# The high and low parts of one portion's first layer, made by GpSimd

## The reference

```
a = x_t @ Wx + b + h @ Wh;   i, f, o = sigmoid(...), g = tanh(...)
c = f * c + i * g;   h = o * tanh(c)              # 64 steps, one after another
z = relu(s0 * [h, -h] @ sign(k0)) * 2             # 512 -> 1024
z = relu(s1 * z @ sign(k1)) * 2                   # 1024 -> 1024
out = x + s2 * z @ sign(k2)                       # 1024 -> 256
```

## Time and profile before

| | |
|---|---|
| runs | 275.78 median, 275.46 to 276.33 |
| the profiled execution: span | 274.2 us; its records give no time beside the span |
| mean granted TensorE clock | 1.000 |
| TensorE matmul busy | 268.8 us, 98% |
| VectorE busy | 219.3 us, 80% |
| ScalarE busy | 174.3 us, 64% |
| GpSimd busy | 40.7 us, 15%, 62 instructions |

### The profile page before, as it was taken

The page is one execution under the profiler, slowest core; times in us unless marked ns, Lnnn a source line. Parts: engine busy times, 40 slices in busy tenths (PEclk is TensorE's granted clock), DMA queues, the critical chain, the costliest instruction groups (busy, mean ns, idle before and its releaser), DMA issues.

```text
span 274.2 us, 8895 instructions
## 1 busy us (share of the span) xinstructions
PE 268.8 (98%) x3568; PEld 219.2 (80%) x3568; DVE 219.3 (80%) x777; ACT 174.3 (64%) x522; POOL 40.7 (15%) x62
## 2 busy tenths in 40 slices
PE   8999999999999999999999999999999999999995
PEld 5887888788999998999988999998777677655663
DVE  3878888888888888888887888886888787998355
ACT  4798787878566666556756565667677667733320
POOL 0010000022111124211311101000200004703030
PEclk9999999999999999999999999999999999999999
DMA  7980000000000001000010001000100000100003
GB/s 199 337 352 1 4 2 0 2 4 2 2 2 1 4 2 41 2 2 5 5 39 0 4 2 41 2 2 5 41 0 2 2 4 0 41 0 0 2 0 115
DMA packets 5432, 8.72 MB, mean 32 GB/s; under 512 B 656, under 2 KB 3472, under 8 KB 5264
## 3 DMA queue, kind: packets, MB, share of 16 engines
q1 hardware_dynamic: 5104, 7.64, 8.2%
q10 hardware_dynamic: 288, 0.52, 0.6%
HBM read 6.07 MB, written 2.10 MB: 30 GB/s over the span
## 4 chain that ended last, share of the span: by engine, by line
PE 85%; DVE 7%; ACT 5%; DMA 1%; issue 1%; ACTq 0%
PE WK L533 27%; PE WK L516 14%; PE G L495 10%; PE WK L551 9%; PE G L486 9%; PE ACC L565 6%; PE G L551 4%; PE WK L582 2%; ACT tT L790 2%; DVE aT L1009 2%; PE ACC L582 1%; DMA x<-in_x 1%; PE G L516 1%; DVE xw L848 1%; ACT xw L688 1%; PE ACC L516 1%
## 5 line engine op out<-in xcount | busy, mean ns | idle before, releaser
L533 PE MATMUL WK<-h,k 128*128 128x256 f16 (+1 forms) x856 | 107.7, 276 | 0.0
L533 PEld LDWEIGHTS WK<-h,k 128*128 128x128 fp8e5 x856 | 80.8, 98 | 10.8
L790 ACT ACTIVATE tT<-aT 128x128 f32<-128x128 f32 x126 | 38.9, 310 | 46.8 <-DVE aT L1009 45.1
L1009 DVE TENSOR_REDUCE aT<-G 128x128 f32<-128x256 f32 x128 | 48.1, 417 | 5.7 <-PE G L495 4.2
L677 ACT ACTIVATE G<-xw 128x256 f32<-128x256 f32 x126 | 46.7, 370 | 0.0
L516 PE MATMUL WK<-xs,wxs 128*128 128x512 f32 x168 | 42.5, 400 | 0.0
L486 PEld LDWEIGHTS G<-h,w 128*128 128x128 f16 x1008 | 32.0, 96 | 10.7 <-DVE h L1026 9.6
L495 PE MATMUL G<-h,w 128*128 128x64 f16 x1008 | 39.5, 192 | 0.0
L486 PE MATMUL G<-h,w 128*128 128x32 f16 x1008 | 35.3, 177 | 1.2 <-DVE h L1026 0.9
L516 PEld LDWEIGHTS WK<-xs,wxs 128*128 128x128 f32 x168 | 30.4, 188 | 5.9
L495 PEld LDWEIGHTS G<-h,w 128*128 128x128 f16 x1008 | 33.2, 97 | 0.0
(11 more groups left out here) (116 smaller groups left out, 281.0 us busy)
## 6 DMA issues: line engine op xcount, KB each, us to landing
x<-in_x SPq DMA_DIRECT2D x3, 512.0 KB, 8.5
out_y<-x SPq DMA_DIRECT2D x10, 128.0 KB, 1.8
xw<-in_wh SPq DMA_DIRECT2D x4, 256.0 KB, 5.2
k<-in_k SPq DMA_DIRECT2D x1, 1024.0 KB, 10.4
out_y<-x SPq DMA_DIRECT2D x4, 192.0 KB, 1.9
x<-in_x ACTq DMA_DIRECT2D x2, 256.0 KB, 3.7
xw<-in_wx SPq DMA_DIRECT2D x4, 128.0 KB, 4.1
xw<-in_wx SPq DMA_DIRECT2D x2, 256.0 KB, 5.4
```

The lines of the kernel that those rows point to most:

```text
L533: ins = eng.matmul(layer_src(tile), w, rhs, start=a == 0, stop=last)
L790: eng.activation(tT[:, B * j0:B * j1], aT[:, j0:j1].rearrange("p j b -> p (j b)"), ACT.Tanh, scale=half_gain0 if t == 0 else half_gain).th ...
L1009: eng.tensor_reduce(aT[:, j0:j1], G[g][:, 0:256].rearrange("p (j h b) -> p j b h", h=2, b=B), op=ALU.add, axis=AX.X).then_inc(added[g])
```

## The change

For the eight first-layer tiles of portion 5, ScalarE reads the bank once, for r1 in f32, and nothing else reads it. GpSimd makes from r1 the high part (a copy to f16) and then the low part (r1 less the high part). TensorE's products p1 and p2 wait for the new semaphore r1_lo, and the next owner of a bank waits for r1_made. In the planner such a tile counts as emptied when it is finished, its pair stands in GpSimd's list one step later, and p1 and p2 are ready from the step after that. In GpSimd's list of step 53 the pairs of tiles 0 and 1 stand behind the two y additions. The pair waits for r1 alone, not for a point of the recurrence.

```
-            inputs = (0, N1, a // 2) in emptied
+            inputs = (0, N1, a // 2) in paired
-            inputs = (0, N1, 4 + a // 2) in emptied and ("p1", tile[1]) in emptied
+            inputs = (0, N1, 4 + a // 2) in paired and ("p1", tile[1]) in emptied
...
+        paired.update(pool[t])
         for tile, at in finished:
-            if tile[0] in ("x", "p1", "y"):
+            if tile[0] in ("x", "p1", "y") or tile[:2] == (0, N1):
                 emptied.add(tile)
-            if tile[0] == "y":
+            if tile[0] == "y" or tile[:2] == (0, N1):
                 pool[t + 1].append(tile)
...
-                    e.wait_ge(lo_made[0], 8 * N1 + 4 * (q - 1) + k + 1)
+                    e.wait_ge(r1_lo, 4 * (q - 1) + k + 1)
...
+                elif old[0] == 0 and old[1] == N1:
+                    e.wait_ge(r1_made, old[2] + 1)
...
                     eng.activation(r1[:, m], layer_src(tile), ACT.Relu).then_inc(r1_made)
+                    return
...
+            def r1_pair(m):
+
+                eng.wait_ge(r1_made, m + 1)
+                eng.tensor_copy(b1[:, m, 0], r1[:, m]).then_inc(r1_hi)
+                eng.wait_ge(r1_hi, m + 1)
+                eng.tensor_tensor(b1[:, m, 1], r1[:, m], b1[:, m, 0], ALU.subtract).then_inc(r1_lo)
+
             for t in range(T):
                 if 0 <= t - MIX_STEP < MIXES:
                     mix_part(t - MIX_STEP)
-                for _, c, mo in pool_plan[t]:
-                    eng.wait_ge(hl_made, t + 1)
-                    y_add(c, mo)
+                for kind, c, m in pool_plan[t]:
+                    if kind == "y":
+                        eng.wait_ge(hl_made, t + 1)
+                        y_add(c, m)
+                    else:
+                        r1_pair(m)
```

More of the change, by code:

```diff
@@ L151, in make_plan @@
     emptied = {("x", 0, j) for j in range(NJ)}
-    todo = []
+    todo, paired = [], set()
     ahead = 0.0
@@ L387, in lstm_ffn @@
         acc_mm, y_out, y_made = ([sem(f"{n}{mo}") for mo in range(2)] for n in ("acc_mm", "y_out", "y_made"))
-        mixed, r1_made, p1_made, n2_mm, r12_made, hi22, lo22 = (
-            sem(n) for n in ("mixed", "r1_made", "p1_made", "n2_mm", "r12_made", "hi22", "lo22"))
+        mixed, r1_made, r1_hi, r1_lo, p1_made, n2_mm, r12_made, hi22, lo22 = (
+            sem(n) for n in ("mixed", "r1_made", "r1_hi", "r1_lo", "p1_made", "n2_mm", "r12_made", "hi22", "lo22"))
         prod_mm = {q: sem(f"prod_mm{q}") for q in range(1, 8)}
```

## The result

The changed kernel has a median of 278.0 us (277.32 to 278.15, four runs) beside 275.7 for the kernel before on the same chip: a ratio of 1.007, 95% interval 1.0054 to 1.0086. It is 0.7% slower. 276.3 was forecast for the likeliest case, with 274.2 to 277.7 as the range; the ratio puts the time at the range's upper end, the bare median 0.3 above it.

The account below looks back on a forecast made before the run. TensorE bounds the kernel, with 2.2 us of waits for the recurrence in steps 53 to 60. Gains of 2.25 less GpSimd's hold-ups in steps 54 and 59 gave 28.1 against 27.6, +0.5: 276.3 us, range 274.2 to 277.7.

Parts of the forecast that it names:

- the case with the largest chance of its own: The main forecast for the whole kernel: a small loss, 276.3 us, own range 275.5 to 277.0, chance 0.50.
- slow cast: Steps 56 to 58: with GpSimd's cast at 0.59 us, L1018 comes 0.1 late, at most +0.3 over the steps.
- The gain: Steps 53 to 60: work taken from VectorE and ScalarE saves 2.25 us if GpSimd's work were free.
- A pair's length: GpSimd's cast (0.48), wait on its own semaphore (0.06) and subtraction (0.92) cost 1.46 us, at most 1.6.
- One pair in a step hidden: Steps 56 to 58, pairs 3 to 5: L1015 is blocked for 0.3 us, but L1018 waits for its tanh anyway.
- Step 54: GpSimd's queued pairs hold up VectorE's recurrence instructions in turn: effective length 5.1 us, +1.84 over 3.26.
- rival (A): Step 54: all six recurrence instructions lose to GpSimd's six; 6.0 us, kernel 277.5 with the +0.3; chance 0.28.
- Step 59: Pairs 6 and 7 ready together; the second holds L1018 and L1020: 4.1 us, +0.9 over 3.20, bounds 3.8 and 4.15.
- (B): Casts don't hold VectorE up, subtractions do; step 54 at 3.7, step 59 at 3.55, kernel 274.3; chance 0.12.
- (C): GpSimd's pairs cost the recurrence nothing in any step: -2.25 us, kernel 273.5; chance 0.10.
- The place at 14.22: Trace of before: L843 takes 1.07 us against 0.68 beside GpSimd casts, read as casts holding VectorE up.

Follow-up runs that it names:

- e1: The changed kernel with GpSimd's eight pairs left out, so p1 and p2 multiply zeros: 273.68 us, ratio 0.9925 to the kernel before.
- e6: The changed kernel with pairs 0 to 6 one per step, none in step 54, tile 7's parts made as in the kernel before: 273.87 us, ratio 0.9914.
- e9: The changed kernel with two one-column memsets between each pair's cast and subtraction: 275.49 us, ratio 0.9986 to the kernel before, on another chip.
- e8: The changed kernel with 15 matmuls of zeros in TensorE's two waits of step 55: 276.95 us, ratio 1.0032 to the kernel before.
- e5: The kernel before, nothing taken away, with GpSimd's eight pairs added into a spare tile nobody reads: 279.91 us, ratio 1.0142.
- e7: The changed kernel as it is, measured a second time: 277.40 us, ratio 1.0052 to the kernel before.
- e2: The changed kernel with each GpSimd pair replaced by three memsets that read nothing: 273.82 us, ratio 0.9928 to the kernel before.

## Why the prediction came out as it did

The forecast was a small loss, hardly to be told from none (+0.5 us); the measured loss is three to four times that (0.5 and 0.7% of 276). The mechanism was right, and the order of chances too (slower 0.42, the largest); the size was not, and the case with the largest chance of its own (0.50, 275.5 to 277.0) isn't the one that came. The top of its range isn't added up: 5.1, 4.15 and the 0.3 of a slow cast give 276.6.

- The gain, -2.25: e1 has 25.39 for the 25.4 forecast, and -2.2 us in its median. TensorE's order was unchanged, as followed in the prediction: `make_plan` of both kernels gives the same list for TensorE in every step, and both traces have 3,568 matmuls.
- A pair's length, 1.46: the cast took 0.50 (0.48 assumed), the subtraction 0.91, from 193.55 to 195.04 in all 1.49. The next pair's cast begins 0.05 ahead of that end.
- One pair in a step hidden: right. Pairs 4 and 5 lie in steps 57 and 58, which take no more than TensorE's need, and L1019 loses at most 0.1. Pair 3 fell into the long step 55 here; e6 has it in a step of its own, at no cost.
- Step 54, the term that failed in size. The prediction wrote 5.1 and named 6.0 for the case in which L1026 loses too; I had it and the subtraction within 0.05 us and gave rival (A) 0.28. Measured is rival (A) in every one of its six turns: 191.82 to 198.06, less the 0.41 at which the second half belongs, 5.83. e9 shows how near such a race is: 0.08 us of delay turned that of L1024. The rows of before could have settled it: a held-up VectorE instruction ends about 0.08 behind GpSimd's and the next starts 0.03 later, 0.11 in all, while GpSimd's wait on its own semaphore was put at 0.06 and took 0.08. I had these figures and still let VectorE win the one race that mattered.
- Step 59: 4.1 forecast, 3.90 measured. L1024 takes 0.96, as forecast, but ends at 3.30 of the step in place of 3.49: the two pairs came 0.2 earlier, the first cast at 0.29 for 0.45, the second at 1.73 for 1.93.
- Not in the sum, nor in any rival: the clock. Two waits of 1.37 and 0.87 us came with a fall to the lower level in six of twelve executions, worth about 1 us in those (1.65 in the traced step 55, 5.79 for 4.14). In the trace it is what comes on top of the mechanism's own price: with the clock up steps 53 to 60 take 28.70 (e8), +1.1 over before and 0.6 under rival (A)'s 29.3, which had the slow cast's 0.3 and 4.1 for step 59 in it. That (A)'s 277.5 and the measured time agree is in part luck. The trace of before never showed a clock below 1.00 in this stretch, but also never a wait of that length; a case that makes TensorE wait for 2 us should have carried a term for it.
- Rivals (B) and (C), casts or all of GpSimd harmless: out, by the first two lines of step 54 and by e5. The place at 14.22 said less for casts than the prediction made of it: L843 ends at 15.29, 0.14 sooner than the casts' end plus its own work (14.75 + 0.68).

The Trainium skill ("SBUF — State Buffer", section Who interferes with whom) says that a VectorE instruction with two SBUF inputs contends with a GpSimd one that reads SBUF, not with one that only writes it, and that tensor_scalar in a two-port mode contends with GpSimd at large. Here both hold, with numbers: 0.22 beside a memset and 0.96 beside a subtraction for L1024; 0.49 beside a cast and 0.29 beside a memset for L1026 (that it ran in such a mode no run shows). Its remark that issue order decides agrees with e9, where L1025 started 0.03 ahead of the subtraction and kept its 0.23.

## What to carry to other kernels

Moving work to an idle engine is free only in the places where it cannot meet the critical chain; here seven pairs cost nothing (e6, 273.87, beside e1's 273.68 without any), and all eight, placed otherwise, 3.7 us. Place elementwise work of GpSimd by the VectorE instructions with two SBUF inputs that run beside it, start it behind the last of them with an explicit wait, and never let two jobs queue up: in step 54 a queue without a pause took one turn for each VectorE instruction of the chain. And when a case makes TensorE wait as long as here (1.4 and 0.9 us in a row), price the clock as well.

## What was not expected of the hardware

- TensorE's clock fell after waits of 1.37 and 0.87 us in the changed kernel's profiled execution, and in another kernel (e5) not after 1.41 and 0.87. In e7's, with waits of 1.36 and 0.87, it was still 1.00 up to 199.00 and fell in the microsecond behind that, when TensorE had been at work again since 198.44. What tips it stays open.
- Two memsets of one column, less than 0.1 us of delay, took about 2 us off the kernel (275.49 for 277.4 to 278.0, 0.7 to 0.8% by the ratios of the chips).
- A tensor_scalar of 64 columns is held up by a GpSimd memset, which reads nothing (0.29 for 0.19, one place in e2), while instructions with two inputs are not.
